# A post-norm block with chunked retention and a gated FFN on one core: the plain fp32 work of a slot gathered in one stretch, and Wo a tile later

## The reference

```
q, k = rotary(x @ Wq) / 8, rotary(x @ Wk);  v = x @ Wv
per head, in chunks:  attn = (q k^T) * gamma^(i-j) for i >= j
                      o = attn @ v + (q * gamma^(i+1)) @ S
                      S = gamma^C * S + (k * gamma^(C-1-j))^T @ v
o = o * rsqrt(mean(o^2) + eps) * gn_weight
x1 = layernorm(x + (o * silu(x @ Wg)) @ Wo)
out = layernorm(x1 + ((silu(x1 @ Wgate^T) * (x1 @ Wup^T)) @ Wdown^T))
```

## Time and profile before

| | |
|---|---|
| median of 3 runs | 427.51 us |
| the profiled execution | 427.98 us |
| its span | 426.1 us |
| TensorE busy | 417.9 us (98%), 4311 products |
| DVE, ACT, POOL busy | 311.6, 258.8, 188.5 us |
| share of TensorE in the chain that ended last | 96% |

### The profile page before, as it was taken

How to read it: one execution, slowest core, us unless ns; L and a number is a source line. 1 busy time by engine, 2 the same in 40 slices (tenths; PEclk the granted TensorE clock), 3 DMA queues, 4 the chain that set the end, 5 groups by cost and what they waited for, 6 DMA issues and landing times.

```text
span 426.1 us, 12403 instructions
## 1 busy us (share of the span) xinstructions
PE 417.9 (98%) x4311; PEld 396.2 (93%) x4311; DVE 311.6 (73%) x905; ACT 258.8 (61%) x795; POOL 188.5 (44%) x331
## 2 busy tenths in 40 slices
PE   8999999999999999999999999999999999999993
PEld 6899999999999999999999999999999999999993
DVE  4999677678676677667778666677767678677774
ACT  6568755577566657566656566656666657555560
POOL 2532343445544345444344544344544344443573
PEclk9999999999999999999999999999999999999999
DMA  8931010201111011111101111011110000100011
GB/s 273 352 142 52 0 52 1 66 0 38 38 40 38 2 40 38 38 37 37 32 5 37 37 37 37 0 37 37 37 37 13 24 16 15 38 14 3 14 37 54
DMA packets 14183, 19.66 MB, mean 46 GB/s; under 512 B 1472, under 2 KB 9664, under 8 KB 14144
## 3 DMA queue, kind: packets, MB, share of 16 engines
q1 hardware_dynamic: 14144, 19.14, 13.8%
HBM read 14.94 MB, written 4.19 MB: 45 GB/s over the span
## 4 chain that ended last, share of the span: by engine, by line
PE 96%; DMA 2%; DVE 0%; SPq 0%; issue 0%; ACT 0%; DVEq 0%
PE b_rows L453 29%; PE b_ffn L453 21%; PE b_rows L471 13%; PE b_rows L467 8%; PE b_head L629 7%; PE b_head L599 3%; PE b_turn L663 3%; PE b_head L595 3%; PE b_ffn L618 3%; PE b_state L648 2%; PE b_turn L481 2%; DMA wf_int<-in_w_proj 1%; DMA out<-wf_int 1%; DVE wf_int L1349 0%; PE b_ffn L648 0%; PE b_ffn L519 0%
## 5 line engine op out<-in xcount | busy, mean ns | idle before, releaser
L1682 POOL TENSOR_TENSOR h_lo<-wf_int,h_hi 128x256 fp32r<-128x256 f32 x96 | 70.8, 739 | 97.3 <-ACT h_hi L995 97.0
L453 PE MATMUL b_ffn<-x1T_hi,wf_hi 128*128 128x256 f32 x384 | 92.7, 278 | 0.0
L453 PE MATMUL b_ffn<-x1T_lo,wf_hi 128*128 128x256 f32 x384 | 92.1, 277 | 0.0
L453 PEld LDWEIGHTS b_ffn<-x1T_hi,wf_hi 128*128 128x128 f32 x384 | 72.2, 188 | 0.6 <-DVE wf_int L1327 0.4
L453 PEld LDWEIGHTS b_ffn<-x1T_lo,wf_hi 128*128 128x128 f32 x384 | 72.2, 188 | 0.0
L970 ACT ACTIVATE sq<-b_head 128x128 f32<-128x128 f32 x124 | 34.5, 278 | 50.5 <-PE b_head L629 47.5
L995 ACT CAST h_hi<-wf_int 128x256 fp32r<-128x256 f32 x96 | 38.8, 404 | 40.5 <-DVE wf_int L1327 39.9
L1700 POOL TENSOR_TENSOR ve<-mv,eps 128x1 f32<-128x1 f32 x64 | 13.9, 216 | 87.7 <-DVE mv L1437 70.9
L471 PE MATMUL b_rows<-wp_hi,xT_lo 128*128 128x256 f32 x198 | 50.0, 277 | 0.0
L1327 DVE TENSOR_TENSOR wf_int<-b_ffn,wf_int 128x256 f32<-128x256 f32 x96 | 40.4, 420 | 11.8 <-ACT wf_int L984 9.0
L984 ACT ACTIVATE wf_int<-b_ffn 128x256 f32<-128x256 f32 x96 | 36.7, 382 | 15.8 <-PE b_ffn L453 14.0
(11 more groups left out here) (152 smaller groups left out, 1224.5 us busy)
## 6 DMA issues: line engine op xcount, KB each, us to landing
xT_raw<-in_xT SPq DMA_DIRECT2D x16, 256.0 KB, 2.7
x_sb<-in_x SPq DMA_DIRECT2D x16, 256.0 KB, 2.7
out<-wf_int SPq DMA_DIRECT2D x32, 128.0 KB, 1.7
wf_int<-in_w_ffn SPq DMA_DIRECT2D x6, 384.0 KB, 6.7
wf_int<-in_w_proj SPq DMA_DIRECT2D x6, 256.0 KB, 4.7
rope_sb<-in_rope SPq DMA_DIRECT2D x4, 256.0 KB, 5.8
rope_q<-in_rope_by_row SPq DMA_DIRECT2D x2, 512.0 KB, 9.5
wo_raw<-in_w_o SPq DMA_DIRECT2D x1, 512.0 KB, 6.3
```

The source lines that it names most:

```text
L453: mm = pe.matmul(dst, a, b, start=(i == 0 and j == 0 and not begun), stop=(i == n - 1 and j == len(passes) - 1 and not more), skip_group_c ...
L1682: pool.tensor_tensor(h_lo[:, ring, hb], h_full[:, u], h_hi[:, ring, hb].bitcast(F32), ALU.subtract).then_inc(h_split[j], 1)
```

## The change

- From slot 9 on (`merged`), TensorE's order is: v; keys and queries; gate-up blocks 0 and 1 of slot s-1; Wo, now of tile s-3 (`wo_lag`); gate-up block 2; down; g; and one plain stretch (`stretch`): k of tile s turned, into b_state; y of tile s-2 turned; retained part and recall of tile s-1; scores and state update of tile s; x1 of tile s-3 turned.
- The retained part comes ahead of recall, and the scores of tile s are computed in slot s rather than in s+1. The wait for the copied k, the finished q and v is put ahead of the last retained product.
- The state has two buffers. g has no products of 512 columns any more.
- Slot 8 (`middle_slot`) keeps its first plain stretch and has Wo, k turned, retained part, scores and update at its end. Slot 9 has no Wo.
- ACT, DVE and POOL get new lists for slots 8, 9 on, and the drain.
- In the drain the steps are in a new order; one recall is left for it, and no scores.

```
@@ tensor engine @@
-            row_stages = [(0, v_copied), (DOWN_LAG + 1, z2_ready), (0, rot_parts), (0, g_gated), (2, z1_ready)]
+            row_stages = [(0, v_copied), (0, rot_parts), (3, z1_ready), (DOWN_LAG + 1, z2_ready), (0, g_gated)]
-                    mm = projection_passes(dst, stat, mov, (2, 0, 3)[c] if natural(s) else (None, 2, 3)[c])
+                    mm = projection_passes(dst, stat, mov, (2, 0, 3)[c] if natural(s) else (None, 2, 0 if merged(s) else 3)[c])
+            def turn_k(s, q, t):
+                pe.wait_ge(rotated, s + 1)
+                pe.wait_ge(state_kept, states_to(*back(q, t, 1)))
+                for b in range(2, 4):
+                    mm = pe.transpose(b_state[:, b * P:(b + 1) * P], qk[:, t % 2, b * P:(b + 1) * P], ident[:])
+                mm.then_inc(qkT_done, 1)
+            def stretch(s, q, t):
+                n, tn = s - 1, back(q, t, 1)[1]
+                def heads_and_state():
+                    pe.wait_ge(qkT_kept, s + 1)
+                    pe.wait_ge(q_rotated, s - 7 if t % 2 else s - 6)
...
+                turn_k(s, q, t)
+                if is_slot(s, NATURAL):
+                    retain(s, q, t, last_waits=heads_and_state)
+                    scores(s, t, False)
+                else:
+                    turn_y(s, q, t)
+                    retain(s, q, t, begun=False, last_waits=heads_and_state, more=tn > 0)
+                    if tn > 0:
+                        recall(n, tn, True).then_inc(o_done, 1)
+                    scores(s, t, True)
+                add_update(s, t)
+                if not is_slot(s, NATURAL):
+                    turn_x1(s, q, t)
+            def merged_slot(s, q, t, wide):
+                project(s, q, t, 1, v_done)
+                keys_and_queries(s, q, t)
+                gate_up_block(s - 1, q, t - 1, 0, wide)
+                gate_up_block(s - 1, q, t - 1, 1, wide)
+                attention_out(s, q, t)
+                gate_up_block(s - 1, q, t - 1, 2, wide)
+                down(s - 1, q, t - 1, wide)
+                project(s, q, t, 2, g_done)
+                stretch(s, q, t)
@@ scalar engine, slot 8 @@
                 turn_q(s, q, t, 1)
+                turn_first_q()
                 split_h(s - 1, t - 1, 2)
...
+                keep_k(s)
+                gate_v(s, q, t)
@@ scalar engine, slots 9 on @@
+                if not is_slot(s, NATURAL + 1):
+                    split_x1T(*prev)
+                mean_squares(*prev)
+                copy_v(s, q, t)
+                keep_x1(s, q, t)
+                if exists(s + 3):
+                    split_xT(s + 3, *back(q, t, -3))
+                gate(s - 1, t - 1, 0)
+                turn_q(s, q, t, 0)
+                gate(s - 1, t - 1, 1)
+                split_h(s - 1, t - 1, 0)
+                turn_q(s, q, t, 1)
+                split_h(s - 1, t - 1, 1)
+                gate(s - 1, t - 1, 2)
+                split_h(s - 1, t - 1, 2)
+                keep_k(s)
+                split_y(s, q, t)
+                gate_v(s, q, t)
@@ vector engine, slots 9 on @@
+                if not is_slot(s, NATURAL + 1):
+                    split_x1T(*prev)
+                add_lower(s, q, t)
+                add_upper(s, q, t)
+                mask(s, q, t)
+                rotate_k(s, q, t)
+                rotate_q(s, q, t)
+                moments_2(s - DOWN_LAG - 2, back(q, t, DOWN_LAG + 2)[1], waited=True)
+                hidden(s - 1, t - 1, 0)
+                sum_k(s, q, t)
+                hidden(s - 1, t - 1, 1)
+                gated_output(*prev)
+                residual_1(s, q, t)
+                hidden(s - 1, t - 1, 2)
...
+                finish_q(s, q, t)
+                residual_2(*prev)
+                stats_2(*prev)
+                norm_1(s, q, t)
+                norm_2(*prev)
+                split_y(s, q, t)
@@ tensor engine, end of the drain @@
-                down(*at(3), wide, (0, 1, 2), free=(z2_ready, NT - 4))
-                down(*at(4), wide, (0, 1, 2), free=(z2_ready, NT - 3))
-                down(*at(5), wide, (0, 1, 2), free=(z2_ready, NT - 2))
+                down(*at(3), wide, (1, 2))
+                down(*at(4), wide, (0, 1), free=(z2_ready, NT - 3))
+                down(*at(5), wide, (0,), free=(z2_ready, NT - 2))
+                down(*at(4), wide, (2,))
+                down(*at(5), wide, (1, 2))
```

More of the change, by code:

```diff
@@ L579, in free_heads, with q_of, recall, scores @@
                         pe.wait_ge(y_ready, 2)
+            def q_of(n, tn, h):
+                if natural(n):
+                    return qkT[half(h), h // 2]
+                return qT[half(h), tn // 2, h // 2, (tn % 2) * P:(tn % 2 + 1) * P]
+            def recall(n, tn, begun):
+                for h in range(H):
+                    for i in range(2):
+                        mm = pe.matmul(o_of(n, h)[half(i)], q_of(n, tn, h)[:, half(i)],
+                                       state[half(h), ring_of(n, tn - 1), h // 2], start=not begun and h < 2,
+                                       stop=begun, skip_group_check=True)
+                return mm
+            def scores(n, tn, begun):
+                for h in range(H):
+                    for j in range(2):
+                        mm = pe.matmul(scores_of(n, h)[half(j)], qkT[half(h), 2 + h // 2, half(j)],
+                                       q_of(n, tn, h), start=not begun and h < 2, stop=True, skip_group_check=True)
+                mm.then_inc(scores_done, 1)
             def recall_and_score(s, q, t):
[L583 to L586, removed]
                 n, (qn, tn) = s - 1, back(q, t, 1)
@@ L592, in recall_and_score @@
                     if tn > 0:
[L593 to L602, removed]
+                        recall(n, tn, False)
+                    scores(n, tn, tn > 0)
             def turn_x1(s, q, t):
@@ L778, in slot @@
                 to_projections(s, q, t, wide)
-                if not is_slot(s, NT - 1):
+                if is_slot(s, NATURAL):
+                    attention_out(s, q, t)
+                    stretch(s, q, t)
+                else:
                     gate_up_block(s, q, t, 0, wide)
@@ L964, in mean_squares @@
                     act.wait_ge(o_done, n + 1)
+                    if not natural(n + 1) and exists(n + 1):
+                        act.wait_ge(scores_done, n + 2)
                     if exists(n - 2):
@@ L1420, in residual_1 @@
             def residual_1(s, q, t):
-                n, (qn, tn) = s - 2, back(q, t, 2)
-                if exists(n):
+                n, (qn, tn) = s - wo_lag(s), back(q, t, wo_lag(s))
+                if exists(n) and not is_slot(s, NATURAL + 1):
                     dve.wait_ge(wo_done, n + 1)
```

360 lines of the change are left out of this document (204 added, 156 removed).

## The result

The changed kernel takes **433.56 us**, the median of 4 runs (433.45 to 433.77), against 427.53 for the kernel before on the same chip (427.02 to 427.81): a ratio of 1.0133 (95% interval 1.011 to 1.0157). It is slower by 1.3%. My prediction was 428.2 with a range up to 430.0, so the result lies outside. The profiled execution took 433.77 us, with a span of 432.0.

The account below looks back on a forecast made before the run. TensorE bounds the kernel: its product steps, its waits and the last tile's path to memory. Terms -0.90 - 0.66 + 0.32 + 0.80 + 1.15 - 0.40 + 0.40 sum to +0.71, giving 428.2 us against the median, range 425.6 to 430.0.

Parts of the forecast that it names:

- Slots 9 to 31: In these slots: counts of products, transposes and small tiles unchanged, only g shorter; 23 slots, -0.9 us (0 to -1.8).
- g: The g product in each slot from 9 on: losing its three wide products saves 0.03 us, 0.04 with settling.
- x1 wait: In eleven short slots: the new order puts v, k and q ahead of x1's first use; -0.66 us, 0 at worst.
- Slot 8: Wo waits for ACT's q copy (+0.37 us), the last retained product for the first q block (+0.43); together +0.80 (0.5 to 1.2).
- Slot 9: Down waits for ACT's last q copy: 0.91 us, plus 0.12 restart and 0.1 longer steps; +1.15 (+0.6 to +1.5).
- Waits in the stretch: From slot 10 on: copied k is ready before the product that carries its wait; cost 0, 0.3 us to spare.
- Drain: After the slots: the new order shortens waits that summed to 0.8 us; -0.4 us, between -0.8 and +0.4.
- Tail: Behind the last product: last residual 0.46 us later, a store's landing may hold tile 28's normalisation; +0.4 us (0.3 to 1.3).
- The cheap pair: Rival: entering the 64-row stage from plain work loses nothing, 23 x 0.15 = 3.4 us saved, 424.8 us; chance 0.15.
- Late q copies in every slot: Rival: one more ACT operation ahead of the q copies makes a wait, times 22, +4.4 us, 432.6 us; chance 0.10.
- The clock: Rival: TensorE runs at the 1.2 GHz level in the long plain stretch, 74 us more, 502 us; chance 0.02.
- full slots under 12.85: Sign of a wrong forecast, pointing to the cheap pair: full slots were forecast 12.93 us apart.

Follow-up runs that it names:

- run 4: Changed kernel with the q block from tile 9 on computed with xT as weights and w_proj moving, q not coming out turned: 428.65 us, ratio 1.0027.
- Runs 1: Changed kernel with the 6 q products put before the 6 k products in every slot from tile 9 on: 434.42 us, ratio 1.017.
- run 6: Changed kernel with q's weights read from a copy of their own starting at byte 192 of 256: 429.12 us, ratio 1.0037.
- run 9: Control: changed kernel with q's weights read from a copy starting at byte 128 of 256, as in the changed kernel: 434.59 us, ratio 1.0172.
- run 3: Kernel before with only g's three wide products taken apart from tile 9 on: 427.16 us, ratio 1.0006.
- run 10: On top of run 6, in slot 9 alone ACT makes the last q copy ahead of the second gate-up block's silu: 428.94 us, ratio 1.0035.
- run 7: Kernel before without its unused 64 B pad, so most split products' weights start 64 B earlier, at byte 128 of 256: 438.2 us, ratio 1.0244.
- runs 5: Changed kernel with q's weights read from a copy of their own starting at byte 0 of 256: 429.36 us, ratio 1.0034.
- run 8: Changed kernel with q's weights read from a copy of their own starting at byte 64 of 256: 429.77 us, ratio 1.0053.

## Why the prediction was wrong

- **The step that failed** is the term *Slots 9 to 31*, priced at -0.9 us because "the number of products, transposes and small tiles stays as it is". It took a split product to cost 0.113 us wherever it stands. I had seen that "products then go every 0.118 for much of the drain" and left it there. The runs show that the step also depends on the order of the blocks: behind q, as its operands lie, it is 0.118 until the 64-row stage. Before, q stood last ahead of that stage in three slots of four, so it cost nothing; in the fourth seven products paid (203.29 to 204.12, 0.118 each, 0.03 us too much). The new order puts 60 products between q and that stage: +0.27 in each of 21 slots, 5.7 us of the 6.0 by which slots 10 to 30 missed; run 4, without q's form, gives 5.8 back. Runs 1, 4, 6 and 9 show it.
- The mechanism of the other parts held. Without the slow steps (run 4) slots are within 0.02 of my 12.93 and 12.48, and slots 10 to 30 differ from the kernel before by -1.29 (267.27 - 268.56) where I had -1.50.
- g: -0.04 a slot was forecast. Run 4's full slots are 0.03 shorter than those before (12.94 for 12.97), so it was about right; in the order of before it is worth -0.02 (run 3).
- x1 wait, -0.66: it is gone, as forecast, but it was not all of the 0.66. In slots such as the one from 198.20 to 210.77 before (12.57 for 12.53) the excess is the seven slow products behind q; six of the eleven short slots are of that kind, some 0.2 us. With q's weights moved (run 6) short slots are 12.54 to 12.55 apart (from 122.42 to 134.97), full ones 12.98, 0.05 to 0.07 over my 12.48 and 12.93, and 0.04 over run 4: q's own slow steps (0.02) and the first gate-up products (0.02).
- Slot 8: Wo waited, and so did the last retained product. Timeline of PE of the changed kernel, last g product, Wo, retained part with its wait inside (the scores follow at 95.93):

```profile
92.58 0.28 PE L480 MATMUL b_rows<-wp_hi,xT_lo 128*128 128x256 f32 x1
92.99 0.36 PE L462 MATMUL b_rows<-wo_hi,yT_hi 128*128 128x256 f32 x1
...
94.67 1.33 PE L658 MATMUL b_head<-v_sb,attn 128*128 128x128 f32 x8
```

  Wo is 0.41 behind g's last product, 0.30 too much, and restarts 0.08 slower: 0.38 (forecast 0.37). The retained part takes 1.33 for 1.06: 0.27 (forecast 0.43).
- Slot 9, the wait of down. Timeline of PE and ACT:

```profile
103.68 0.39 PE L462 MATMUL b_rows<-wf_hi,h_hi 128*128 128x256 f32 x1 [0.54 <-ACT q_turn L988]
...
103.26 0.36 ACT L988 COPY q_turn<-b_rows 32x256 f32<-32x256 f32 x1
```

  The copy ends at 103.62, and down starts 0.06 later. Its delay of 0.71 with 0.11 of restart is 0.82 for my 0.91 + 0.12 + 0.1; gate-up block 2 waited another 0.16 with 0.11 of restart, which I had not seen. Together 1.09 for 1.15. The place and, by run 10, the cause of the wait of down were right. That the size came out is luck: down's part was 0.3 too large, and a wait that I had not seen made it up.
- Waits in the stretch: none, as forecast (the retained part and recall follow without a gap, below). Drain: -0.4 forecast, -0.31 measured once the 1.36 of the Wo that moved into it is taken off; which of its waits went and which came was not followed up.
- Tail: the step itself held, its price didn't. The last residual stands 0.75 behind the last product (425.75 to 426.50, DVE below) against 0.32 before (419.37 to 419.69), so 0.43 later for my 0.46. But the stores' landings, which held the last normalisation for 0.76 before, held it for 0.43, and from that normalisation's end to the end of the span it is 3.07 for 3.82 before; so -0.48 in place of +0.40.

```profile
426.50 0.42 DVE L1578 SCALAR_TENSOR_TENSOR wo_raw<-b_rows,wf_int 128x256 f32<-128x256 f32 x1
...
428.03 0.90 DVE L1470 TENSOR_SCALAR wf_int<-wo_raw,mv,rs 128x256 f32<-128x256 f32 x2 [0.43 <-DMA out<-wf_int]
```

- Rivals. The cheap pair: no. The first recall stands 0.99 behind the first of eight retained pieces (223.89 to 224.88), and 8 x 0.109 = 0.87, so entering from plain work costs 0.12, no less than the 0.10 from split work. The Trainium skill's page "TensorEngine Tiling (Array Packing)", Key Properties, says that a change of tiling mode drains the engine and makes no exception for a kind of data; the trace agrees. Late q copies in every slot: no, only in slot 9. That rival's time, 432.6, lay nearest to the result by luck: the result has nothing to do with q copies. The clock: granted 0.998, no.

I had also named the sign that would prove me wrong as "full slots under 12.85", a wait, or no gap in slot 9. Full slots at 13.20 with no wait in them had no place in my list. The lower end of the range, 425.6, is also not "halfway to the cheap pair" (424.8) from 428.2, which would be 426.5; it played no part in the miss.

## What to carry to other kernels

Before pricing a new order at "the same products", divide distances by counts in several places of the trace. If one kind of product has two steps there (here 0.113 and 0.118), find out what stands ahead of each; 4.5 ns were worth 1.3% of this kernel. An odd pad between buffers may be a tuned one. Here the use that breaks its pattern (q, with its operands in swapped roles) cost least where it stood last ahead of the 64-row stage. Waits can be forecast to 0.1 or 0.3 us from rows, as those of slots 8 and 9 were, and still be the small part.

## What the runs showed of the hardware

- The step of a split product of 256 columns depends on where its weights and moving rows start within 256 B: 0.113 us at 192 and 128, 0.120 at 128 and 128 (run 7, Wo), 0.114 at 128 and 64 (run 7, down), 0.117 in the q block with weights at 0 or 192 and rows at 192 (runs 5 and 6), 0.120 with weights at 64 (run 8), 0.113 with 128 and 192 (the changed kernel). That the place counts modulo 256 B is borne out by run 9 alone, where a copy far away but at the same byte of 256 behaves as the original does.
- It also depends on what went ahead. After the block with 128 and 192, products that otherwise step at 0.113 go at 0.118, for 60 in a row, across changes of bank and across wide products; the 64-row stage ended it in each of slots 10 to 30. After a q block that is slow itself they are back at 0.113 within a few products.
- A q block is not the only thing that does it: a wait can too. In the drain of the kernel before there is no q block, yet behind the wait of the earlier trace rows 35 steps take 4.13, 0.118 each. Timeline of PE before, the second product behind that wait and a down product:

```profile
408.37 0.28 PE L453 MATMUL b_ffn<-x1T_lo,wf_hi 128*128 128x256 f32 x1
...
412.50 0.28 PE L453 MATMUL b_rows<-wf_hi,h_hi 128*128 128x256 f32 x1
```

  A wait can also end it, without any 64-row stage: in slot 9 of the changed kernel steps are 0.118 up to the wait of down at 103.68, and from 104.25 to 106.52 twenty of them take 2.27, 0.1135 each. In run 10, where down waits no more, g in that slot stays at 1.42 / 12 = 0.118. And in the drain before, nine steps from 418.35 to 419.37 are at 0.113 again, a few products behind a wait at 417.55. So this looks like a state that a q block or a wait can put the engine into and that a wait or the 64-row stage can end.
- Why is open. Only the place of q's weights and the pad were varied, and no run shows what the engine does with such a pair or in such a wait.
- Not tried: moving xT for q from a second copy at byte 128, which would give q the places of all the others, but costs ACT and POOL a second split of each tile.
